# A DLRM tower on one core: full-height id spreads, ten bf16 zeros products, and the last tile's pairs taken chunk by chunk

## The reference

```python
# tables e[f] are (rows, 128); 10 of the 26 fields have 1000 or 1250 rows and are "one-hot" fields here
e = jnp.stack([tbl_0[ids[:, 0]], ..., tbl_25[ids[:, 25]]], axis=1)      # (512, 26, 128)
combined = jnp.concatenate([e, r_dense_x[:, None, :]], axis=1)          # (512, 27, 128)
interact = jnp.einsum('bfd,bgd->bfg', combined, combined)
z = interact[:, TRIU_I, TRIU_J]                                         # (512, 351)
h = jnp.concatenate([z, r_dense_x], axis=1)                             # (512, 479)
h = jnp.maximum(h @ W_top1 + b_top1, 0.0)                               # 512 wide
h = jnp.maximum(h @ W_top2 + b_top2, 0.0)                               # 256 wide
y = h @ W_top3                                                          # (512, 1)
```

## Time and profile before

| what | us |
|---|---|
| median of 3 runs | 112.58 |
| the three runs | 110.67, 112.70, 112.58 |
| the profiled execution | 110.61 |
| its span, first to last instruction | 108.8 |
| busy: TensorE products, VectorE, ScalarE, GpSimd | 101.8, 80.2, 75.4, 62.8 |

### The profile page before, as it was taken

One profiled execution on the slowest core, in us unless ns is written; L12 is line 12 of the kernel. 1 busy time (PEld: TensorE's weight loads), 2 busy tenths in 40 slices (PEclk: granted clock), 3 DMA queues, 4 the chain that ended last, 5 costly groups with the idle time before them and its releaser, 6 DMA issues.

```text
span 108.8 us, 2593 instructions
## 1 busy us (share of the span) xinstructions
PE 101.8 (94%) x994; PEld 79.9 (73%) x994; DVE 80.2 (74%) x161; ACT 75.4 (69%) x148; POOL 62.8 (58%) x72
## 2 busy tenths in 40 slices
PE   5999999989999999999898977999999989799992
PEld 1447567655766656688577967999999979798991
DVE  5599999979999999999972783489337932386210
ACT  4599379999999999999945762376527732376320
POOL 3777777777777777776777777777776000000000
PEclk9999999999999999999999999999999999999999
DMA  2854649994563817551112222122221100000000
GB/s 45 336 200 69 227 90 409 369 304 78 214 182 116 256 39 262 125 215 48 48 48 60 66 54 48 48 54 65 60 50 48 30 0 0 6 0 0 0 6 1
DMA packets 5199, 11.64 MB, mean 107 GB/s; under 512 B 1978, under 2 KB 2490, under 8 KB 5188
## 3 DMA queue, kind: packets, MB, share of 16 engines
q1 hardware_dynamic: 3120, 7.27, 20.2%
q0 software_dynamic: 2048, 4.20, 14.6%
q10 hardware_dynamic: 20, 0.02, 0.1%
HBM read 11.48 MB, written 0.00 MB: 106 GB/s over the span
## 4 chain that ended last, share of the span: by engine, by line
PE 89%; DVE 5%; issue 2%; ACT 1%; DVEq 0%
PE gram_ps L556 39%; PE gram_ps L591 13%; PE tr_ps L572 6%; PE act_ps L625 5%; PE dve_ps L625 4%; PE top_ps L636 3%; PE tr_ps L673 3%; DVE pairs L470 2%; PE dve_ps L532 2%; PE tr_ps L667 2%; PE gram_ps L532 2%; PE top_ps L660 2%; PE gram_ps L612 1%; PE tr_ps L625 1%; PE act_ps L532 1%
## 5 line engine op out<-in xcount | busy, mean ns | idle before, releaser
L280 POOL DMA_INDIRECT rows<-table,ids_sb x64 | 61.9, 967 | 20.7 <-issue 19.2
L556 PE MATMUL gram_ps<-onehot,high 128*128 128x512 f32 x82 | 23.2, 429 | 1.0 <-issue 1.0
L556 PE MATMUL gram_ps<-onehot,low 128*128 128x512 f32 x82 | 21.4, 404 | 0.0
L556 PEld LDWEIGHTS gram_ps<-onehot,high 128*128 128x128 f32 x82 | 15.3, 201 | 7.4 <-issue 3.6
L556 PEld LDWEIGHTS gram_ps<-onehot,low 128*128 128x128 f32 x82 | 14.7, 188 | 6.1 <-issue 3.4
L294 ACT ACTIVATE xt<-gram_ps 128x512 f32<-128x512 f32 x10 | 12.0, 1202 | 4.9 <-PE gram_ps L556 4.9
L591 PE MATMUL gram_ps<-xt 128*58 128x52 f32 x512 | 14.5, 217 | 0.9 <-DVE xt L429 0.6
L443 DVE TENSOR_TENSOR onehot<-dve_ps,row_f 128x1024 fp32r<-128x1024 f32 (+1 forms) x10 | 14.4, 1484 | 1.2 <-PE act_ps L532 1.2
L591 PEld LDWEIGHTS gram_ps<-xt 128*58 128x58 f32 x512 | 14.0, 133 | 1.6 <-DVE xt L429 0.8
L455 DVE TENSOR_TENSOR low<-table,high 128x256 fp32r<-128x256 f32 (+1 forms) x40 | 14.5, 426 | 0.8 <-ACT high L372 0.6
L443 DVE TENSOR_TENSOR onehot<-gram_ps,row_f 128x1536 fp32r<-128x1536 f32 (+1 forms) x10 | 14.9, 1536 | 0.0
(11 more groups left out here) (72 smaller groups left out, 106.5 us busy)
## 6 DMA issues: line engine op xcount, KB each, us to landing
table<-table SPq DMA_DIRECT2D x9, 512.0 KB, 3.9
rows<-table,ids_sb POOLq DMA_INDIRECT x64, 3.0
w1p_sb<-w_pairs SPq DMA_DIRECT2D x1, 768.0 KB, 5.6
table<-table SPq DMA_DIRECT2D x1, 640.0 KB, 4.1
w_sb<-w SPq DMA_DIRECT2D x1, 512.0 KB, 7.0
dense_sb<-dense SPq DMA_DIRECT2D x1, 256.0 KB, 4.9
w1d_sb<-w_dense SPq DMA_DIRECT2D x1, 256.0 KB, 5.9
ids_sb<-ids SPq DMA_DIRECT2D x1, 52.0 KB, 1.9
```

Of the source, the lines that this page charges most:

```text
L280: pool.indirect_dma_start(rows[:, t, s - 1, :], None, tables[f], bass.IndirectOffsetOnAxis(ids_sb[:, t, f:f + 1], 0)).then_inc(gathered[t] ...
L556: last = pe.matmul(pick_ps[b][:], weights[:, c, :], onehot[:, b, c, :], start=(c == 0 and part == 0), stop=(c == CHUNKS[o] - 1 and part == 1))
```

## The change

1. `select` and `field_ids16` are now 128 rows high instead of 10; the other 118 rows of `field_ids16` are set to zero by a new VectorE memset between `select` and the conversion of the ids, and the conversion waits for it. `spread` is unchanged in text, and its products now have 128 by 128 weights. `field_of`, made by GpSimd's iota, has 128 rows too.
2. The three fp32 zeros products of 256 columns between `spread(0)` and `spread(1)` become ten bf16 zeros products of 512 columns.
3. In the last tile the transposition of the last slot stands ahead of `first_layer(2, (3,))` instead of behind it.
4. The end of the last tile is re-cut. TensorE does all of `dense_part(3)` ahead of the transpositions, transposes the packed chunks one at a time in the order 2, 1, 0, each when the rectangles that it needs are packed, then multiplies chunk by chunk (chunk 2 with all four column blocks, then 1, then 0), and `third_layer(2)` moves behind that. ScalarE packs rectangles 8, 7, 6, copies chunk 2 out, packs 5 and 4, copies chunk 0, and only then evacuates `second_layer(2)`; VectorE copies chunk 1.

```diff
 DVE_PARTS = 3
-WARM_UP = (4, 3)
+WARM_UP = (4, 10)
 WEIGHTS_AFTER = 3
...
 ACT_RECTS_LATE = [5, 4]
+LAST_CHUNKS = (2, 1, 0)
+assert rect_at(7) <= 2 * P and rect_at(5) <= P and rect_at(6) >= P
 EARLY_J = RECTS[6][0] - 1
...
         row_of = sb("row_of", [P, MAX_CHUNKS], I32)
-        field_of = sb("field_of", [NO, NO], I32)
+        field_of = sb("field_of", [P, NO], I32)
         row_f = sb("row_f", [P, MAX_CHUNKS])
...
         field_ids = sb("field_ids", [NO, B], I32)
-        field_ids16 = sb("field_ids16", [NO, B], F16)
-        select = sb("select", [NO, NO, P], F16)
+        field_ids16 = sb("field_ids16", [P, B], F16)
+        select = sb("select", [P, NO, P], F16)
         onehot = sb("onehot", [P, 2, MAX_CHUNKS, B], F32R)
...
         h1_ps_last = [act_ps[:, 0:P], tr_ps[1][:, 0, :], dve_ps[:, 0:P], tr_ps[0][:, 0, :]]
+        back_ps_last = [gram_ps[2][:, 0:P], gram_ps[1][:, 0:P], gram_ps[0][:, 0:P]]
         h2_ps = [top_ps[:, 0, :], top_ps[:, 1, :]]
...
         select_ready = sem("select_ready")
+        ids16_zero = sem("ids16_zero")
         ids16_ready = sem("ids16_ready")
...
+            def back_last(c, n):
+                act.wait_ge(last_back_ready, n)
+                act.activation(pairs_t[:, c, :], back_ps_last[c], ACT.Copy).then_inc(last_back_out[c], 1)
+
             def first_layer(n):
...
                 step(t, True)
-            pack(TILES)
+            act.wait_ge(pairs_ready, 2 * TILES)
+            for r in ACT_RECTS_EARLY:
+                last = act.activation(*rect(r), ACT.Copy)
+                if r == 7:
+                    last.then_inc(last_packed_act, 1)
+            back_last(2, 1)
+            act.wait_ge(pairs_ready, 2 * TILES + 1)
+            for r in ACT_RECTS_LATE:
+                act.activation(*rect(r), ACT.Copy).then_inc(last_packed_act, 1)
+            back_last(0, 3)
             second_layer(TILES - 1)
-            back(TILES)
-            third_layer(TILES - 1)
             for k, m in enumerate((0, 1)):
...
                 act.activation(h1[:, m, :], h1_ps_last[m], ACT.Relu, bias=b1_sb[:, m:m + 1]).then_inc(h1_out_act, 1)
+            third_layer(TILES - 1)
             act.wait_ge(h2_ready, TILES)
...
             dve.tensor_scalar(select[:], field_of[:].rearrange("k (o p) -> k o p", p=1
-                                                               ).to_broadcast([NO, NO, P]),
-                              row_f[0:NO, 0:1], None, ALU.is_equal).then_inc(select_ready, 1)
+                                                               ).to_broadcast([P, NO, P]),
+                              row_f[:, 0:1], None, ALU.is_equal).then_inc(select_ready, 1)
+            dve.memset(field_ids16[:], 0.0).then_inc(ids16_zero, 1)
             dve.wait_ge(field_ids_in, 16)
-            dve.tensor_copy(field_ids16[:], field_ids[:]).then_inc(ids16_ready, 1)
+            dve.wait_ge(ids16_zero, 1)
+            dve.tensor_copy(field_ids16[0:NO], field_ids[:]).then_inc(ids16_ready, 1)
...
             pack(TILES)
-            back(TILES)
+            dve.wait_ge(last_back_ready, 2)
+            dve.tensor_copy(pairs_t[:, 1, :], back_ps_last[1]).then_inc(last_back_out[1], 1)
             for k, m in enumerate((2, 3)):
...
+            def back_last(c):
+
+                if c == 2:
+                    pe.wait_ge(last_packed_act, 1)
+                elif c == 1:
+                    pe.wait_ge(last_packed_act, 2)
+                else:
+                    pe.wait_ge(last_packed_act, 3)
+                    pe.wait_ge(packed_dve, TILES)
+                pe.transpose(back_ps_last[c], packed[:, c * P:(c + 1) * P], ident[:]).then_inc(last_back_ready, 1)
+
+            def first_layer_last(c, last):
+
+                pe.wait_ge(last_back_out[c], 1)
+                for m in (0, 2, 1, 3):
+                    made = pe.matmul(h1_ps_last[m], w1p_sb[:, c, m * P:(m + 1) * P], pairs_t[:, c, :],
+                                     start=False, stop=last, skip_group_check=True)
+                    if last:
+                        made.then_inc(h1_ready, 1)
+
             def h1_banks(t):
...
             spread(0)
-            zeros_f = zeros[:].bitcast(F32)
             for _ in range(WARM_UP[1]):
-                pe.matmul(tr_ps[1][:].rearrange("p s n -> p (s n)")[:, 0:B // 2], zeros_f[:, 0:P], zeros_f, start=True,
-                          stop=True)
+                pe.matmul(tr_ps[1][:].rearrange("p s n -> p (s n)"), zeros[:, 0:P], zeros[:], start=True, stop=True)
             spread(1)
...
                     transposes(t, range(4, NT))
-                first_layer(t - 1, (1, 3))
+                first_layer(t - 1, (1,))
                 if t == TILES - 1:
                     transposes(t, range(4, NT))
+                first_layer(t - 1, (3,))
                 gram(t)
             second_layer(TILES - 2)
-            dense_part(TILES - 1, (0, 2))
-            back(TILES - 1)
-            dense_part(TILES - 1, (1, 3))
+            dense_part(TILES - 1, (0, 2, 1, 3))
+            for c in LAST_CHUNKS:
+                back_last(c)
+            for c in LAST_CHUNKS:
+                first_layer_last(c, c == LAST_CHUNKS[-1])
             third_layer(TILES - 2)
-            first_layer(TILES - 1, (0, 2, 1, 3))
             second_layer_last(TILES - 1)
...
```

More of the change, by code:

```diff
@@ L201, in tower @@
         packed_act = sem("packed_act")
+        last_packed_act = sem("last_packed_act")
+        last_back_ready = sem("last_back_ready")
+        last_back_out = [sem(f"last_back_out{c}") for c in range(NC)]
         back_ready = sem("back_ready")
```

## The result

The changed kernel took 109.18 us as a median of 4 runs (109.15 to 109.23). The kernel before, run beside it, took 111.62 us as a median of 4 runs: two at 110.67 and two at 112.58 and 112.70. Against the runs of before at 110.67 the ratio is 0.9866, 95% interval 0.9842 to 0.9889: 1.3% faster. By the 2% that the prediction takes as the smallest clear difference that is "the same", to which it gave 0.44 against 0.48 for faster. The profiled execution took 109.18 us with a span of 107.4, against 110.61 and 108.8.

The account below looks back on a forecast made before the run. TensorE's low clock at the start, then ScalarE's pace in the picks until VectorE binds, plus last-tile waits, were taken as limits. Sum: 110.61 - 0.9 (clock) - 0.52 (slot) + 0.44 (end) = 109.6 us; range 108.3 to 112.2.

Parts of the forecast that it names:

- All its signs: Timeline: starts 0.22 to 0.25 apart before the first pick, shorter ScalarE wait, last gram without idle, second_layer_last some 10.6 behind.
- The early clock's gain: First table's picks: low products end at 13.3 instead of 14.25, 0.9 us gained at ScalarE's wait.
- the rise at 7.7: Start, TensorE: the clock goes from 1.2 to 2.4 GHz at 7.7, with about 8.2 zeros done.
- the bound of 6.9: Start, TensorE: earliest clock rise, after 3.6 us of unbroken full-height work counted from 3.26.
- a bound of about 1.4 at the fifth table: Picks: VectorE's one-hots for the fifth table's chunk 2 allow at most about 1.4 us of gain there.
- The ten zeros: Between spreads: all at the low clock they end at 8.47, alone delaying the picks by 1.6 us.
- The memset: Start, VectorE: conversion of the ids 0.17 late, bounds 0 and 0.4; VectorE regains 0.58, 0.41 net.
- The slot's transposition: Last tile: moved ahead of the last column block, the gram starts at about 93.29, 0.52 us gained, bounds 0.4 and 0.57.
- The end: End of last tile: second_layer_last would follow at 104.42 instead of 103.98, 0.44 us lost, bounds 0.1 and 0.65.
- The exposed third layer: End of last tile: third_layer(2), hidden beside the copies before, now follows the first layer and takes 0.36.
- The late start of the first layer: End of last tile: rectangles 5 and 4 wait behind chunk 2's copy; first layer starts at 101.38 instead of 101.22.
- the estimate of 112.4: Upper runs of before: first table's low products still at the low clock, 1.75 us lost against the profiled execution.

Follow-up runs that it names:

- The padding experiment: Changed kernel with the four memsets of xt's padding kept on VectorE but moved out of the picks: 108.40 us.
- the four nearest to it: Changed kernel with one edit each: last tile's end as before 108.85, slot's transposition as before 109.58, three fp32 zeros 109.24, ids' memset on GpSimd 108.95 us.
- ids' memset: Changed kernel with the memset of the ids moved from VectorE to GpSimd, ahead of its gathers: 108.95 us.

## Why the prediction was right

The time (109.18 against 109.6), its sign and its size hold, and so does the main line: taller spreads bring the rise ahead of the first pick, and that brings the first gram forward. The experiment with 10-row spreads and ten zeros shows it by changing the height alone. All its signs came, `second_layer_last` 10.44 behind the last gram where it said 10.6. That the sum is within 0.45 us owes a little to luck: the clock's gain (0.53 too small) and the end's loss (0.09 too large) err one way, the slot's gain (0.17 too large) the other.

The prediction weighed a rule of the Trainium skill ("TensorE: Matmul & The Clock Gate", Part 1: The HAM clock gate), that matmul activity releases the clock, and left open whether spreads or zeros fail it. Zeros agree with the rule: with 10-row spreads the rise came behind 4.4 us of them. The 10-row spreads fit it badly: TensorE was at work from 1.19, with at most 0.26 of pause, in all three profiles that have them, and the clock rose at 7.61, near 8.65 and at 11.71.

**The early clock's gain** is the term that was mis-sized, 0.9 against 1.43, and two things in it were off. The first is the rise at 7.7. Nine profiles have tall spreads with zeros between them and no long pause at the start: in six the clock rose at 4.6 to 4.9, in three at 6.4 to 6.8. All lie ahead of the bound of 6.9, which took only the work from 3.26 on; so the zeros from 1.19 on may have told as well, but no run tests that, and since one start gave 4.73 and 6.36, the program alone does not fix the time. The second is what limits the gain. The prediction let ScalarE's wait for the first pick set it and kept VectorE as a bound of about 1.4 at the fifth table. VectorE was the limit all the way: 48.67 us of work without a wait, started 0.2 late by the memset. So the bound was near and the rise did not matter for the rest: 4.73, 6.36 and, in the kernel before, 7.61 give the same first gram but for VectorE's start. The padding experiment, which takes work from VectorE, brings that gram 0.83 further forward.

**The ten zeros** were priced as a delay of the picks that the early clock repays. In the changed kernel's profile they delay nothing, since the picks wait for ScalarE's high copy, which ends at 7.08; where the clock rose at 6.36 the picks started half a us later, and VectorE hid it. Three fp32 zeros give 109.24; with none the time rises (109.27 to 110.64).

**The memset** was put at 0.17 with VectorE regaining 0.41. It cost 0.23, in full on the path, since VectorE had nothing left to regain behind the early rise.

**The slot's transposition**, 0.52 foretold, brought 0.35 by the traces and 0.40 by its undoing. The missed 0.17 is a wait ahead of the transposition: it needs the bank whose copy ends at 90.92, so it starts at 91.06, 0.19 later than the products ahead of it would allow, and the column block behind it in TensorE's queue is held up with it.

**The end**, 0.44 lost foretold, lost 0.35 by the traces and 0.33 by its undoing; at the last second layer, where the prediction put its sum, it is 0.27 (10.44 against 10.17), and the rest is lost behind it. The exposed third layer (0.36) is right. The late start of the first layer (0.16) did not come: ScalarE's copy took 0.28 but rectangle 5 started 0.17 into it, so both remaining chunks went from 99.13 on.

**The groups.** That the runs of before differ by the time of the rise is shown for two groups, and the estimate of 112.4 for the upper one was near. What the prediction did not see is a third group at 108.9; the profiled execution of before, which it took for one with an early rise, belongs to the middle group. Against the lowest group the change loses: the kernel with the end as before and the slot's gain, 108.85, is within 0.1 of it. So where the clock rises ahead of the picks the change is 0.23 (memset) + 0.33 (end) - 0.40 (slot) = 0.16 us slower, close to 109.18 - 108.93 = 0.25. What it brings is that the rise comes in time in every run: 109.15 to 109.23, and in 42 runs of this kernel and the four nearest to it (end, slot, zeros, ids' memset) none lies more than 0.1 from its kernel's median.

## What to carry to other kernels

When a kernel's runs fall into groups, look for the time at which the matmul starts tighten in each, before tuning anything behind it: small products of few rows between warm-up products can put the rise off, and filling their rows with zeros costs no time on TensorE (the two products of a spread start 0.38 apart either way), though here the memset cost 0.23 us on VectorE. How early the rise has to come is set by the engine that binds next; earlier than that brings nothing. A move that fills an idle gap on one engine is worth what the next engine's chain leaves; here VectorE set the limit, and ScalarE stood hardly a microsecond behind. Re-cutting a short tail into pieces pays only if no engine's queue has to wait in the middle for a piece, and if what used to hide in the gap does not end on the path.
